# A sorted-edge graph kernel: in every third group the source rows of two tiles come from one-hot products on TensorE

## What is computed

```python
x, y = h[src], h[dst]
msg = einsum('eb,ebo->eo', w_comp[etype], einsum('ei,bio->ebo', x, weight))   # 16 bases
x_hat = x @ A1_w.T + A1_b
y_hat = y @ A2_w.T + A2_b + rel_emb[etype]
a = tanh(relu(sum(x_hat * y_hat, -1) / sqrt(32)))
nei = segment_sum(a[:, None] * msg, dst)
curr = h[src[last edge of the node]] @ self_loop_weight
h_new = relu(nei + curr) where the node has an edge, else 0
```

## Time and profile before

| | |
|---|---|
| runs | 1391.6, 1391.75, 1392.74 us, median 1391.75 |
| the profiled execution | 1394.01 us, its span 1392.1 us |
| PE busy | 1022.2 us (73% of the span) |
| PEld busy | 910.9 us (65%) |
| DVE busy | 922.9 us (66%) |
| ACT busy | 661.8 us (48%) |
| POOL busy | 757.2 us (54%) |
| mean granted TensorE clock | 0.651 |

### The profile page before, as it was taken

How to read it: one execution, slowest core, us unless ns; L and a number is a source line. 1 busy time by engine, 2 the same in 40 slices (tenths; PEclk the granted TensorE clock), 3 DMA queues, 4 the chain that set the end, 5 groups by cost and what they waited for, 6 DMA issues and landing times.

```text
span 1392.1 us, 43827 instructions
## 1 busy us (share of the span) xinstructions
PE 1022.2 (73%) x16664; PEld 910.9 (65%) x16664; DVE 922.9 (66%) x3162; ACT 661.8 (48%) x1721; POOL 757.2 (54%) x793
## 2 busy tenths in 40 slices
PE   3268888878767776776776677667737794999995
PEld 2257777767656655665666566556627693999995
DVE  7277888887666666666666667677634875555555
ACT  1156666665555555555555556455577860000000
POOL 5777777777777777777777777777600000000000
PEclk9555555665555555555555555555558897999998
DMA  4521111121111111111111111111000000000000
GB/s 103 80 57 46 41 39 38 39 45 45 46 37 36 43 38 34 34 41 39 35 34 42 38 33 34 44 39 26 14 12 3 3 3 1 4 4 4 4 4 16
DMA packets 60199, 44.58 MB, mean 32 GB/s; under 512 B 43584, under 2 KB 56224, under 8 KB 59984
## 3 DMA queue, kind: packets, MB, share of 16 engines
q1 hardware_dynamic: 34960, 28.86, 7.5%
q0 software_dynamic: 25024, 12.86, 6.2%
HBM read 38.58 MB, written 3.07 MB: 30 GB/s over the span
## 4 chain that ended last, share of the span: by engine, by line
POOL 41%; PE 27%; issue 15%; DVE 11%; DMA 3%; SPq 1%; ACT 1%; DVEq 0%; ACTq 0%
POOL arena L521 41%; PE ps L708 15%; PE ps L673 4%; PE ps L736 3%; DVE arena L1123 2%; PE ps L731 2%; DVE arena L1121 1%; SPq L424 1%; DMA arena<-line_table 1%; DMA dst_parts<-arena 1%; PE ps L606 1%; DVE arena L1151 1%; DVE arena L1106 1%; PE ps L658 1%; DVE arena L1136 1%
## 5 line engine op out<-in xcount | busy, mean ns | idle before, releaser
L521 POOL DMA_INDIRECT arena<-x_pad,arena x782 | 755.4, 966 | 238.6 <-issue 238.3
L641 PE MATMUL ps<-arena 128*128 128x175 bf16 (+3 forms) x1567 | 193.5, 291 | 157.0 <-DVE arena L1123 156.7
L641 PEld LDWEIGHTS ps<-arena 128*128 128x128 bf16 x1567 | 143.9, 129 | 171.1 <-DVE arena L1123 170.6
L708 PE MATMUL ps<-arena,adj_words 128*128 128x64 f16 (+1 forms) x6875 | 215.5, 193 | 42.7 <-DVEq L1216 22.9
L673 PE MATMUL ps<-mix,arena 128*80 128x32 f32 x1666 | 243.5, 327 | 0.6 <-ACT arena L870 0.6
L708 PEld LDWEIGHTS ps<-arena,adj_words 128*128 128x128 fp8e4 x6875 | 212.9, 98 | 45.5 <-DVEq L1216 23.6
L673 PEld LDWEIGHTS ps<-mix,arena 128*80 128x80 f32 x1666 | 237.0, 234 | 3.0 <-ACT arena L870 1.2
L1123 DVE TENSOR_SCALAR arena<-pair_no,arena 128x275 bf16<-128x275 f16 (+2 forms) x784 | 238.1, 308 | 0.0
L1136 DVE TENSOR_TENSOR arena<-ps,arena 128x132 f32<-128x132 f32 x196 | 57.3, 292 | 251.2 <-DMA arena<-x_pad,arena 156.1
L658 PE MATMUL ps<-arena 128*32 128x187 f32 x1568 | 158.5, 495 | 78.5 <-DVE arena L1151 78.5
L1151 DVE TENSOR_TENSOR arena<-ps,arena 128x768 f32<-128x768 f32 x196 | 187.9, 959 | 6.7
(11 more groups left out here) (187 smaller groups left out, 1108.0 us busy)
## 6 DMA issues: line engine op xcount, KB each, us to landing
arena<-line_table SPq DMA_DIRECT2D x28, 602.0 KB
arena<-x_pad,arena POOLq DMA_INDIRECT x782, 2.5
arena<-line_table SPq DMA_DIRECT2D x28, 140.0 KB
arena<-dst_parts SPq DMA_DIRECT2D x196, 5.7 KB
agg_table<-arena SPq DMA_DIRECT2D x196, 2.5 KB
dst_parts<-arena SPq DMA_DIRECT2D x1, 918.8 KB, 12.1
feat_table<-rows SPq DMA_DIRECT2D x1, 800.0 KB, 14.1
x<-x_pad SPq DMA_DIRECT2D x1, 400.0 KB
```

Source lines behind the costliest of these rows:

```text
L521: pool.indirect_dma_start(to, None, table, bass.IndirectOffsetOnAxis(ap=index, axis=0)).then_inc(done, 16)
L641: mm = nc.tensor.matmul(ps[:, at + d0 * BLOCKS:at + d1 * BLOCKS], row_hot[:, h, k, :], pair_hot[:, h, k, (d0 - first) * BLOCKS:(d1 - first ...
L708: mm = nc.tensor.matmul(ps[:, at:at + cols], adj[:, b, j * P:(j + 1) * P], parts[:, half, b, 0:cols], start=(b == 0), stop=(b == BLOCKS - 1))
```

## The change

In 64 of the 196 groups (3, 6, ..., 192) POOL gathers two tiles instead of four. The rows of the other two are picked from `x`, split into three bf16 parts that lie in SBUF. A source node number is cut into its low 9 bits and the rest. A line of low bits, less 0, 128, 256 and 384, is stored in `src_table` in the prologue; ACT issues a DMA that broadcasts one group's line (1024 fp16 numbers) over 128 partitions; DVE compares it with the partition's number (`make_src_hot`); TensorE multiplies each of the four one-hots with every fourth block of x (`pick`, 24 matmuls a group), which leaves seven candidates a row; DVE selects one of them with a mask and a sum (`select_picks`). `ROWS_BY_SCALAR` becomes 2, so that ACT makes two of the four source one-hots. `AHEAD` becomes 14. The result of times_bases moves to the end of a bank of the sums, to free a bank, and copy_moved comes later in ACT's order. Cut to its core:

```diff
-AHEAD = 21
+AHEAD = 14
-ROWS_BY_SCALAR = 1
+ROWS_BY_SCALAR = 2
+PICK_EVERY, PICKS = 3, 2
+LOW, HIGHS = 4, 7
+LOW_BITS = 9
+SRC_LINES = 2
+SRC_LINE_AHEAD = 7
+PICKED = [g for g in range(PICK_EVERY, GROUPS, PICK_EVERY) if (g + 1) * SLOTS <= TILES]
...
+        src_table = nc.dram_tensor("src_table", [GROUPS, LOW * PICKS * P], F16, kind="Internal").ap()
...
-        COUNTS, FETCHED, MIXED, MOVED, SMALL = [bank * BANK for bank in (0, 2, 4, 6, 7)]
+        COUNTS, FETCHED, MIXED, PICKED_AT, SMALL = [bank * BANK for bank in (0, 2, 4, 6, 7)]
+        MOVED = MIXED + PAGE * MIXES
...
+        def gathered_tiles(g):
+            return min(SLOTS - PICKS if g in PICKED else SLOTS, TILES - g * SLOTS)
...
@@ SP
+                           (src_line, src_rows_in.rearrange("p (g e) -> p g e", g=LINE_GROUPS)[:, :, WINDOW - PICKS * P:])):
...
+            sp.wait_ge(src_lines_made, 1)
+            sp.dma_start(src_table.rearrange("(p g) (j e) -> p g j e", p=LINE_ROWS, j=LOW), src_line_parts)\
+              .then_inc(src_lines_stored, 16)
...
@@ TensorE
+                def pick(g):
+                    n = PICKED.index(g)
+                    pe.wait_ge(src_hot_ready, n + 1)
+                    if n >= 1:
+                        pe.wait_ge(picks_read, n)
+                    for k in range(PICKS):
+                        for low in range(LOW):
+                            rows_in = x_parts[:, :, low::LOW, :]
+                            at, cols = PICKED_AT + k * HIGHS * FEAT, len(range(low, BLOCKS, LOW)) * FEAT
+                            for j in range(3):
+                                mm = nc.tensor.matmul(ps[:, at:at + cols], src_hot[:, n % SRC_LINES, low, k * P:(k + 1) * P],
+                                                      rows_in[:, j], start=(low == 0 and j == 0),
+                                                      stop=(low == LOW - 1 and j == 2))
+                    mm.then_inc(picks_out, 1)
...
                     if g + 1 < GROUPS:
                         fetch(g + 1)
                         count(g + 1)
+                    if g + 2 in PICKED:
+                        pick(g + 2)
                     sum_mixed(g)
...
@@ ACT
                 def copy_sums(g):
                     act.wait_ge(mixed_used, g + 1)
                     c, n = g // BATCH, g % BATCH
                     if n == 0 and c >= 2:
                         act.wait_ge(moved_out, c - 1)
+                    if n == 2 and c >= 1:
+                        copy_moved(c - 1)
...
+                def load_src_line(g):
+                    n = PICKED.index(g)
+                    if n >= SRC_LINES:
+                        act.wait_ge(picks_out, n - SRC_LINES + 1)
+                    a.dma_start(src_lines[:, n % SRC_LINES, :], src_table[g:g + 1, :].to_broadcast([P, LOW * PICKS * P]))\
+                     .then_inc(src_line_in[n % SRC_LINES], 16)
...
                     if g + 2 < GROUPS:
                         make_rows(g + 2)
+                    if g + SRC_LINE_AHEAD in PICKED[SRC_LINES:]:
+                        load_src_line(g + SRC_LINE_AHEAD)
                     copy_counts(g)
                     if g >= 1:
                         copy_sums(g - 1)
-                    if g % BATCH == 2 and g > BATCH:
-                        copy_moved(g // BATCH - 1)
...
@@ DVE, prologue
+            link(v.tensor_scalar(src_line, src_line, (1 << LOW_BITS) - 1, None, ALU.bitwise_and))
+            for low in range(LOW):
+                link(v.tensor_scalar(src_line_parts[:, :, low, :], src_line, float(low * P), None, ALU.subtract))
+            dve.sem_inc(src_lines_made, 1)
...
+            link(v.tensor_scalar(block_of, by_slot, LOW_BITS, None, ALU.logical_shift_right))
...
+            link(v.tensor_tensor(high_hot, hot_no[:, 0:HIGHS].unsqueeze(1).unsqueeze(1).to_broadcast(n),
+                                 high_of.unsqueeze(3).to_broadcast(n), ALU.is_equal))
...
+            dve.wait_ge(src_lines_stored, 16)
...
@@ DVE, sweep
+                split(link, x[:], work[:], [x_parts[:, j] for j in range(3)])
...
+                def make_src_hot(g):
+                    n = PICKED.index(g)
+                    dve.wait_ge(src_line_in[n % SRC_LINES], 16 * (n // SRC_LINES + 1))
+                    v.tensor_scalar(src_hot[:, n % SRC_LINES].rearrange("p j e -> p (j e)"), src_lines[:, n % SRC_LINES],
+                                    side_no[:, 0:1], None, ALU.is_equal).then_inc(src_hot_ready, 1)
+
+                def select_picks(g):
+                    n = PICKED.index(g)
+                    dve.wait_ge(picks_out, n + 1)
+                    if g >= AHEAD:
+                        dve.wait_ge(mixed_used, g - AHEAD + 1)
+                    own = ps[:, PICKED_AT:PICKED_AT + PICKS * HIGHS * FEAT].rearrange("p (s h f) -> p s h f", s=PICKS, h=HIGHS)
+                    link(v.tensor_tensor(picked, own, high_hot[:, n].unsqueeze(3).to_broadcast([P, PICKS, HIGHS, FEAT]),
+                                         ALU.mult))
+                    dve.sem_inc(picks_read, 1)
+                    link(v.tensor_reduce(xp[:, g % AHEAD, SLOTS - PICKS:, 0:FEAT], picked.rearrange("p s h f -> p s f h"),
+                                         AX.X, ALU.add))
...
+                    if g + 3 in PICKED:
+                        make_src_hot(g + 3)
                     make_mixed(g)
+                    if g + 1 in PICKED:
+                        select_picks(g + 1)
```

More of the change, by code:

```diff
@@ L94 @@
 SUM_COLS = {P_REL: FEAT, P_SUM: FEAT + 1, P_SOFT: FEAT + 1, P_OUTDEG: 1, P_PROP: FEAT}
+PICKED = [g for g in range(PICK_EVERY, GROUPS, PICK_EVERY) if (g + 1) * SLOTS <= TILES]
+assert LOW * P == 1 << LOW_BITS and LOW * HIGHS >= BLOCKS
 def rows_of(b):
@@ L260, in gnn @@
         agg_rows = sweep.cut(ROW_PAGES * FEAT, n=BATCH * PAGE).rearrange("p (h f) -> p h f", f=FEAT)
+        src_lines = sweep.cut(SRC_LINES * LOW * PICKS * P, F16)
+        src_hot = src_lines.bitcast(BF16).rearrange("p (h j e) -> p h j e", h=SRC_LINES, j=LOW)
+        src_lines = src_lines.rearrange("p (h e) -> p h e", h=SRC_LINES)
+        x_parts = sweep.cut(3 * BLOCKS * FEAT, BF16).rearrange("p (j b f) -> p j b f", j=3, b=BLOCKS)
+        picked = sweep.cut(PICKS * HIGHS * FEAT).rearrange("p (s h f) -> p s h f", s=PICKS, h=HIGHS)
         nothing = sweep.cut(BANK, BF16, n=1)
@@ L347, in gnn @@
         rows_paged, agg_loaded = sem("rows_paged"), sem("agg_loaded")
+        src_lines_made, src_lines_stored = sem("src_lines_made"), sem("src_lines_stored")
+        src_line_in = [sem(f"src_line_in_{h}") for h in range(SRC_LINES)]
+        src_hot_ready, picks_out, picks_read = sem("src_hot_ready"), sem("picks_out"), sem("picks_read")
         sweep_cleared = sem("sweep_cleared")
@@ L527, in gather_group @@
             def gather_group(g):
-                for t in range(g * SLOTS, min((g + 1) * SLOTS, TILES)):
+                for t in range(g * SLOTS, g * SLOTS + gathered_tiles(g)):
                     gather(xp[:, g % AHEAD, t % SLOTS, 0:FEAT], x_pad, src_t[:, t:t + 1], gathered[g % AHEAD])
@@ L862, in copy_counts, with copy_moved @@
                     act.wait_ge(squared, g + 1)
+                def copy_moved(c):
+                    act.wait_ge(moved_out, c + 1)
+                    if c >= ROW_PAGES:
+                        act.wait_ge(rows_paged, 16 * BATCH * (c - ROW_PAGES + 1))
+                    a.copy(agg_rows[:, c % ROW_PAGES, :], ps[0:BATCH * PAGE, MOVED:MOVED + FEAT]).then_inc(moved_copied, 1)
                 def copy_sums(g):
@@ L871, in copy_sums @@
                            ps[:, at:at + PAGE * MIXES]).then_inc(sumsT_copied, 1)
-                def copy_moved(c):
-                    act.wait_ge(moved_out, c + 1)
-                    if c >= ROW_PAGES:
-                        act.wait_ge(rows_paged, 16 * BATCH * (c - ROW_PAGES + 1))
-                    a.copy(agg_rows[:, c % ROW_PAGES, :], ps[0:BATCH * PAGE, MOVED:MOVED + FEAT]).then_inc(moved_copied, 1)
                 def move_page(g):
@@ L885, in move_page @@
                      .then_inc(pages_moved, 1)
+                def load_src_line(g):
[4 more added lines that the diff above has]
+                     .then_inc(src_line_in[n % SRC_LINES], 16)
+                act.wait_ge(src_lines_stored, 16)
+                for g in PICKED[0:SRC_LINES]:
+                    load_src_line(g)
                 make_rows(0)
@@ L1132, in score_edges @@
                     dve.wait_ge(fetched, g + 1)
-                    tiles = min((g + 1) * SLOTS, TILES) - g * SLOTS
-                    earlier = sum(min((n + 1) * SLOTS, TILES) - n * SLOTS for n in range(g % AHEAD, g, AHEAD))
-                    dve.wait_ge(gathered[g % AHEAD], 16 * (earlier + tiles))
+                    dve.wait_ge(gathered[g % AHEAD], 16 * sum(gathered_tiles(n) for n in range(g % AHEAD, g + 1, AHEAD)))
                     link(v.tensor_tensor(product, fetched_of(g)[:, :, 0:SCORED], xp[:, g % AHEAD], ALU.mult))
```

(2 more changed lines are left out.)

15 lines of the change are left out of this document (11 added, 4 removed).

## The result

The changed kernel takes 1425.99 us (median of 4 runs, 1423.1 to 1426.7), the kernel before 1392.22 (4 runs, 1391.6 to 1392.74): ratio 1.0239, 95% interval 1.0227 to 1.0252. The forecast was 1358. Where a few runs of a kernel took over 1.5% longer than its fastest, its time and ratio here are those of the others. The profiled execution took 1426.7 us, its span is 1424.9.

The account below looks back on a forecast made before the run. It took POOL's gathers as the later sweep's bound; without it, DVE's twelve-group terms sum from 50.6 to 54.7 us, 4.56 a group, last product 974.5 instead of 1009.1, -34 us: 1358 us, range 1308 to 1425.

Parts of the forecast that it names:

- The bound moved off POOL: Sweep: with 128 gathers saved, POOL needs 4.24 us a group, a floor and no longer the bound.
- TensorE's clock: TensorE in the sweep: 40% of the time outside L673 at full clock, PEclk rising to about 0.7.
- Rival 1: TensorE stays at its low clock and bounds the sweep at 4.94 us a group: 1431 us, slower; chance 0.20.
- The pick's length: TensorE: a pick of 24 matmuls takes 3.9 us at the low clock, 2.6 at the full one.
- DVE's own work for four picks: DVE, twelve groups: make_src_hot +1.0 us and select_picks +5.2.
- waits that the pick's matmuls make: DVE, twelve groups: +1.1 us for later fetches and +1.2 for short waits behind picks at the low clock.
- a run of L673 that falls into a fast stretch loses some 2.1 us: TensorE's product with the bases: shorter at full clock; at 40% this takes 2.5 us off twelve groups.
- the next fetch comes up to 1.6 us later: TensorE: one pick in three stands right ahead of sum and L673; with 0.3 for the others, +1.1 us in twelve groups.
- The sign for being wrong at the root: DVE still waits for gathers, or its wait for the fetch (L628) grows past 3.5 us a run.
- Rival 2: Clock mostly full, L673 some 2.7 us, selection hidden in its wait: pace 4.3 us a group, 1307 us; chance 0.18.
- rival 3: DVE's selection costs 1.9 us, or ACT hands weights late: 4.76 us a group, 1396 us, no change; chance 0.12.
- Rival 4: Source lines come late, 2 us each time: 128 us at most, more likely half hidden, 1422 us; chance 0.05.

Follow-up runs that it names:

- two matmuls: The changed kernel with 2 of the 24 matmuls of each pick left (picked rows then wrong): 1340.42 us, 0.9616 of the kernel before.
- the sums side by side: The changed kernel with the weights of L718 stored in adjacent words, ACT's copy doing the striding: 1354.67 us, 0.9714 of the kernel before.

## Why the prediction was wrong

What held, step by step:
- **The bound moved off POOL.** 654 gathers, no wait of DVE for rows, POOL waiting for freed buffers: as written, though its last gather starts at 982.8 us and not by 950, since the pace was slower. The saved row comparison and the start (84.6 for 85.5) too.
- **TensorE's clock.** 0.69 to 0.73 in the sweep's stretches, for a forecast of about 0.7. Rival 1, the low clock throughout, did not occur; that its time, 1431, is the nearest to what was measured is chance.
- **The pick's length.** 4.16 us at the low clock and 2.22 at the full one, for forecasts of 3.9 and 2.6; the mean of the 64 is 3.45.

The ledger for twelve groups, from the forecast's 54.7 to the measured 58.9:

| step, in us for twelve groups | forecast | measured | from |
|---|---|---|---|
| DVE as before, less the row comparison | 48.7 | 48.7 | taken over |
| DVE's own work for four picks | 6.2 | 8.4 | 5.26-3.16, four times |
| L718 faster at full clock | -2.5 | 0 | 4.97 us at both clocks |
| waits that the pick's matmuls make | 2.3 | 5.3 | (4.905-4.46) x 12, two matmuls |
| DVE's own work hidden in the waits for L718 | 0 | -3.5 | what is left |
| sum | 54.7 | 58.9 | |

The last but one row is a remainder, and most of it can be seen: DVE's waits at the three runs of L718 are 2.93, 3.09 and 2.98 us in the early stage before (groups 12 to 59), 9.0 in all, and 6.0 with two matmuls. That is 3.0 of the 3.5.

**The step that failed first is "a run of L673 that falls into a fast stretch loses some 2.1 us."** It was read from another fp32 group, L718 of the kernel before, which doubled its rate. L673 differs in that its weights are 17 words apart, and its rate doesn't follow the clock. The code showed the stride; all runs of L673 in the trace of before stood at the low clock and could show nothing. In the sum it counts 2.5, but the sums side by side gave back 71 us (1425.99 less 1354.67), 4.4 for twelve groups: the forecast had 40% of the time outside L673 at full clock and took that for its runs too, while with the new layout 31 of 49 stood there, each 2.35 us shorter. No dearer pick is needed to explain the difference. The second failed step is "the next fetch comes up to 1.6 us later": pick, sum and L718 are one stretch on TensorE ahead of the fetch, and the step there is 10.2 us with the pick and 7.1 with two of its matmuls, 3.0 more. The sum took less still: 1.6 and twice 0.3 are 2.2, and it has 1.1 without a reason for the half. The waits from picks were 5.3, not 1.1 + 1.2.

**DVE's own work was mis-sized**: make_src_hot compares 1024 columns, not the 512 that it was priced by, 484 ns for 0.26 us; the reduction takes 934 ns for some 0.58. Here the stride was noted and the row from PSUM without one was taken all the same. The estimate from the Trainium skill's figure ("Vector Engine (DVE) Microarchitecture Reference", 5.2 Measured stream behaviour on trn2) was 0.86 us, and the trace is nearer to it than to 0.58: 934 ns strided, 620 side by side. Part of this came back: with two matmuls DVE waits 1.80, 1.01 and 3.15 us at the three runs of L718 instead of some 3.0 each. That its longer own work lies in that wait is the likely reason, not a shown one.

**Its own signs.** No run of L673 ended in under 3 us, as some should have. The sign for being wrong at the root, a wait for the fetch of over 3.5 us a run, did not come: it was 150.2/48 = 3.1 on average, and 4.3 only where the pick stands ahead. The mean hid the place.

**ACT** was nearly as written: 8 us of the result is ACT's wait for the pick ahead of the line.

**Rival 2** came true in part when the sums lay side by side: L718 fell to 2.62 us at the full clock, forecast 2.7. But its 1307 needed a pace of 4.3, and the measured one is 4.53. Of rival 3, the selection took some 1.6 us (621 and 934 ns), between the 1.3 of the sum and its 1.9. Rival 4, late source lines, left no wait in the trace.

## What to carry to other kernels

A rate at the full clock may be carried over from another matmul only if its operands are laid out alike: look at the strides of the weights and the moving rows as well as at type and shape, and if need be let an engine with room (here ACT, 58 us more busy) do the striding. What work added to TensorE costs depends on where it stands: right ahead of another long piece, with the next fetch behind both, a pick of 3.9 us cost 3.0, at its other places 0 to 1.6. Put it away from such a piece; that alone, with as many picks, was 4.9% on the slower chips. And run an experiment beside the kernel before on the same chip, since the same pair of kernels here stands at 1.024 on one chip and at 0.955 on another.

## What was not expected of the hardware

- 34 fp32 passes with weights of 80 columns, 17 words apart: 4.97 us at 1.2 GHz and 4.95 at 2.4, at either 141 ns from start to start. Side by side: 4.74 us at 1.2 and 2.62 at 2.4 GHz, 134 and 72 ns from start to start.
- The pick with a moving operand in steps of four bf16 numbers: 4.64 us at 1.2 GHz and 4.44 at 2.4 for its 24 matmuls, where side by side it takes 4.16 and 2.22.
- ACT's copy of 340 fp32 columns: 445 ns side by side, 743 with an output in steps of 80 words.
- DVE's reduction of 448 fp32 columns in SBUF: 620 ns side by side, 934 with a stride of 32 words.
- The kernel before takes 1392 to 1397 us on some chips and 1668 to 1689 on others, with TensorE idle for "issue" in the middle of a fetch. Why is open.
